# End of a second attention: output path and routing moved earlier, two banks for the products with v, fillers in the late slots

## The reference

```
x = x + attn_a(layernorm(x))      # 16 heads of 8, hyperbolic distances
x = x + ffn(layernorm(x))
x = x + attn_b(layernorm(x))      # 16 heads of 8, rotary, softmax(q k / sqrt(8)) v, projection
x = x + ffn(layernorm(x))

def ffn(x):                       # x: 2048 tokens x 128
    scores = sigmoid(x @ router_w.T); sfc = scores + e_bias          # 64 experts in 8 groups
    group_scores = top_k(sfc by group, 2).sum(-1)
    keep the 4 best groups, then the 8 best experts of those
    w = 2.5 * scores of the 8 / their sum                            # coef, zero elsewhere
    return sum_e (silu(x @ Wg_e) * (x @ Wu_e) * coef_e) @ Wd_e + shared expert
```

## Time and profile before

| what | value |
|---|---|
| median of 3 runs (lowest, highest) | 1089.32 us (1086.78, 1092.47) |
| profiled execution: own time, span | 1086.67 us, 1084.9 us |
| TensorE matmul busy | 971.3 us (90%) |
| VectorE busy | 959.2 us (88%) |
| ScalarE busy | 671.2 us (62%) |
| mean granted TensorE clock | 0.867 of full speed |

### The profile page before, as it was taken

One profiled execution on the slowest core, in us unless ns is written; L12 is line 12 of the kernel. 1 busy time (PEld: TensorE's weight loads), 2 busy tenths in 40 slices (PEclk: granted clock), 3 DMA queues, 4 the chain that ended last, 5 costly groups with the idle time before them and its releaser, 6 DMA issues. The chain is left out here.

```text
span 1084.9 us, 17540 instructions
## 1 busy us (share of the span) xinstructions
PE 971.3 (90%) x5387; PEld 694.7 (64%) x5387; DVE 959.2 (88%) x1447; ACT 671.2 (62%) x848; POOL 368.7 (34%) x266
## 2 busy tenths in 40 slices
PE   6767887878669999999999899899889999999997
PEld 4533444444347888888888555455568888888886
DVE  7799999999988999999999797987589999999997
ACT  4779999999934545445445554876544544545544
POOL 2054666667901433333331211111203333333330
PEclk9865555555669999999999998999789999999999
DMA  2000000000119555555550000112049555555521
GB/s 59 1 1 1 1 1 1 1 1 1 52 30 215 157 160 151 147 157 147 155 153 4 1 1 1 23 23 31 16 107 225 151 147 157 148 154 155 147 85 39
DMA packets 50711, 86.94 MB, mean 80 GB/s; under 512 B 20092, under 2 KB 33404, under 8 KB 50556
## 3 DMA queue, kind: packets, MB, share of 16 engines
q1 hardware_dynamic: 50664, 86.34, 30.6%
HBM read 83.33 MB, written 2.98 MB: 80 GB/s over the span
## 5 line engine op out<-in xcount | busy, mean ns | idle before, releaser
L1514 ACT ACTIVATE sg<-ps 128x512 f32<-128x512 f32 x264 | 156.8, 594 | 264.8 <-PE ps L523 263.2
L523 PE MATMUL ps<-xh,whi 128*128 128x512 f32 x528 | 206.2, 391 | 1.3 <-ACT b L1330 1.3
L523 PE MATMUL ps<-xl,whi 128*128 128x512 f32 x528 | 205.9, 390 | 0.0
L523 PE MATMUL ps<-xh,wlo 128*128 128x512 f32 x528 | 205.8, 390 | 0.0
L2329 DVE TENSOR_TENSOR hf<-sg,ps 128x512 f32<-128x512 f32 x264 | 170.3, 684 | 29.9 <-DVE hl L2336 24.4
L1727 POOL CAST whi<-wraw 128x384 fp32r<-128x384 f32 x66 | 66.3, 1004 | 370.2 <-PE ps L523 285.5
L1647 POOL TENSOR_TENSOR rr<-xr,rr 128x2048 f32<-128x2048 f32 x32 | 145.2, 4569 | 125.0 <-ACT rr L1305 71.2
L2336 DVE TENSOR_TENSOR hl<-hf,hh 128x1024 fp32r<-128x1024 f32 x132 | 178.2, 1350 | 0.8 <-DVE hf L2329 0.8
L2341 DVE TENSOR_TENSOR hf<-hf,cbc 128x1024 f32<-128x1024 f32 x128 | 157.6, 1231 | 13.4
L1542 ACT ACTIVATE hh<-hf 128x1024 fp32r<-128x1024 f32 x132 | 139.2, 1055 | 4.6 <-DVE hf L2341 4.6
L1729 POOL TENSOR_TENSOR wlo<-wraw,whi 128x384 fp32r<-128x384 f32 x66 | 116.3, 1762 | 5.3
(11 more groups left out here) (277 smaller groups left out, 1512.3 us busy)
## 6 DMA issues: line engine op xcount, KB each, us to landing
cbc<-routing_coefficients SPq DMA_DIRECT2D x256, 256.0 KB, 3.8
wraw<-in_wexp_dram SPq DMA_DIRECT2D x66, 192.0 KB, 2.7
X<-in_x_dram SPq DMA_DIRECT2D x4, 256.0 KB, 4.8
routing_coefficients<-cT SPq DMA_DIRECT2D x8, 128.0 KB, 2.3
out_dram<-X SPq DMA_DIRECT2D x4, 256.0 KB, 2.9
heads_by_row<-o_all SPq DMA_DIRECT2D x12, 72.0 KB
b_rows<-heads_by_row SPq DMA_DIRECT2D x12, 72.0 KB, 2.7
rope_in<-in_consts_dram SPq DMA_DIRECT2D x1, 512.0 KB, 3.4
```

The source lines that it names most:

```text
L523: return pe.matmul(o, l, r, start=start, stop=stop, **kw)
L1514: act.activation(sg[c % 2][:, :], bank(4 + 2 * (c % 2)), ACT.Silu).then_inc(s_sg, 1)
```

## The change

Five things are changed, all between slot 42 of the second attention and the start of the second expert loop.

- The output path of chunk 1 (`normalise`, `transposed`, `projected`, `residual`, `stats_of`) moves one to five slots earlier, and fillers are placed anew.
- The two `f_transposed` of half 0 move from U = 53 and 55 to V = 59 and 61 (U = 48 and 50), their copies from VectorE to ScalarE (`copy_xT`), and the logits from U = 56 and 57 to 53 and 54.
- The products with v of the last groups alternate between banks 6 and 2.
- `TAIL_FILL` adds one filler to most slots from U = 55 and two to each of the last three.
- Routing of half 0 is cut into pieces. Sigmoids go by group. `route_masked` to `route_coefs` of half 0 and its `lows` move out of `prepare_f` into `samples_b`, between the steps of chunk 3. `lows` of half 1 comes before its routing, not after. In `last_of_b` TensorE's order changes, and the last copy to `f_xT` goes from ScalarE to VectorE.

The diff, cut where helpers are only moved or renamed:

```diff
@@ -390,6 +391,21 @@
...
+        def logit_bank(f, i, g):
...
+            if f == 0:
+                return bank(spare(f, i, g) + 1)[:, 0:GTILES * E]
+            n, at = ((0, 0), (1, 0), (1, 0), (1, 1))[2 * i + g]
+            return bank(n)[:, at * GTILES * E:(at + 1) * GTILES * E]
...
+        def pair_bank(n):
+
+            return 2 if 2 * n >= LAST_PAIRS and n % 2 else 6
@@ -876,7 +892,8 @@
...
-            WAITS_FOR_PATH = {39: 4, 46: 3, 47: 4, 55: 4, 62: 3, 63: 4}
+            WAITS_FOR_PATH = {39: 4, 46: 3, 47: 4, 54: 4, 57: 2, 58: 3}
+            TAIL_FILL = {55: 1, 56: 1, 57: 1, 58: 1, 60: 1, 62: 1, 63: 1, 64: 2, 65: 2, 66: 2}
@@ -898,6 +915,8 @@
...
+                elif U in TAIL_FILL:
+                    keep_busy(shifted_bank(2 * U) if U <= 61 else 0, TAIL_FILL[U])
@@ -920,10 +939,12 @@
...
-                if s in (4, 6):
-                    pe.wait_ge(s_oTs, B + s // 2 - 1)
-                elif s in (5, 7):
-                    pe.wait_ge(s_ores, B + s // 2 - 1)
+                if s == 4:
+                    pe.wait_ge(s_oTs, B + 1)
+                elif s in (5, 6):
+                    pe.wait_ge(s_ores, B + s - 4)
+                elif s == 7:
+                    pe.wait_ge(s_fxT, GROUPS + 2)
@@ -950,8 +971,11 @@
...
                 if C % 2 == 0 and half == 0 and C >= 2:
-                    pe.wait_ge(s_bev, C // 2)
-                last = pv(vt, s, c, wr[:, C % CHUNKS, :], bank(6)[:, C % 2 * N:(C % 2 + 1) * N], (half,))
+                    if C == LAST_PAIRS:
+                        pe.wait_ge(s_mx, 2 * B * UNITS - 2)
+                    else:
+                        pe.wait_ge(s_bev, C // 2 if C < LAST_PAIRS else C // 2 - 1)
+                last = pv(vt, s, c, wr[:, C % CHUNKS, :], bank(pair_bank(C // 2))[:, C % 2 * N:(C % 2 + 1) * N], (half,))
@@ -993,32 +1017,35 @@
...
-                if V in (38, 54):
-                    c = (V - 38) // 16
+                if V in (38, 53):
+                    c = (V - 38) // 15
                     pe.wait_ge(s_q2, 2 * (V // UNITS))
                     pe.wait_ge(s_on, B + c + 1)
                     transposed(c, 7)
-                elif V in (43, 59):
+                elif V in (43, 55):
                     pe.wait_ge(s_q2, 2 * (V // UNITS))
-                    projected((V - 43) // 16, 7)
+                    projected((V - 43) // 12, 7)
+                elif V == 59:
+                    pe.wait_ge(s_q2, 2 * (V // UNITS))
+                    f_transposed(1, 0, 0)
+                elif V == 61:
+                    pe.wait_ge(s_fxT, GROUPS + 1)
+                    f_transposed(1, 0, 1)
             def b_tail_step(U):
                 if U == 53:
                     pe.wait_ge(s_mx, 2 * B * UNITS - 1)
-                    f_transposed(1, 0, 0)
-                elif U == 55:
+                    logits(1, 0, 0)
+                elif U == 54:
                     pe.wait_ge(s_mx, 2 * B * UNITS)
-                    f_transposed(1, 0, 1)
-                elif U == 56:
-                    logits(1, 0, 0)
-                elif U == 57:
                     logits(1, 0, 1)
                 elif U == 59:
                     pe.wait_ge(s_q2, 2 * B)
                     pe.wait_ge(s_on, B + 3)
                     transposed(2, 7)
                 elif U == 61:
+                    pe.wait_ge(s_sc, lap(1, 0, 1))
                     projected(2, 1)
@@ -1026,30 +1053,23 @@
                 pe.wait_ge(s_bev, 2 * B)
                 token_major(0, 2)
                 token_major(1, 4)
+                keep_busy(6, 2)
+                pe.wait_ge(s_oTs, B + 3)
+                f_transposed(1, 1, 0)
+                keep_busy(6, 2)
                 pe.wait_ge(s_on, B + 5)
                 transposed(3, 2)
-                keep_busy(4, 3)
-                projected(3, 3)
-                f_transposed(1, 1, 0)
                 pe.wait_ge(s_ores, B + 3)
                 logits(1, 1, 0)
-                keep_busy(4, 4)
+                projected(3, 3)
+                keep_busy(4, 6)
                 f_transposed(1, 1, 1)
                 keep_busy(4, 3)
                 logits(1, 1, 1)
...
             def normal_bank(f, i, g):
-                return spare(f, i, g) if f == 0 else (0, 1, 7, 6)[2 * i + g]
...
+                return spare(f, i, g) if f == 0 else (7, 7, 7, 6)[2 * i + g]
@@ -1415,27 +1435,32 @@
...
-                    if U in (27, 43):
-                        o_transposed_b((U - 27) // 16, 7)
-                    elif U == 37:
-                        f_norm_rstd(1, 0)
-                    elif U == 52:
-                        f_norm_rstd(1, 1)
-                    elif U == 58:
-                        logit_exps(1, 0)
+                    if U in (27, 42):
+                        o_transposed_b((U - 27) // 15, 7)
+                    elif U in (37, 47):
+                        f_norm_rstd(1, (U - 37) // 10)
+                    elif U in (48, 50):
+                        copy_xT((U - 48) // 2)
+                    elif U in (54, 55):
+                        logit_exps(1, 0, (U - 54,))
                     elif U == 60:
                         o_transposed_b(2, 7)
                     elif U == B * UNITS:
                         f_norm_rstd(1, 2)
...
+            def copy_xT(g):
+                act.wait_ge(s_fxnT, GROUPS + g + 1)
+                act.activation(f_xT[g][:, :], bank(7), ACT.Copy).then_inc(s_fxT, 1)
+                act.wait_ge(s_fxT, GROUPS + g + 1)
+                f_high(g)
@@ -1451,26 +1476,14 @@
...
             def last_of_b():
-                act.wait_ge(s_fxT, GROUPS + 2)
-                f_high(0)
-                f_high(1)
+                copy_xT(2)
                 o_transposed_b(3, 2)
-                act.wait_ge(s_fxnT, GROUPS + 3)
-                act.activation(f_xT[2][:, :], bank(7), ACT.Copy).then_inc(s_fxT, 1)
                 f_norm_rstd(1, 3)
-                act.wait_ge(s_fxT, GROUPS + 3)
-                f_high(2)
                 f_norm_apply_group(1, 3)
                 act.preload_act_table_set("sigmoid_and_others")
-                act.wait_ge(s_fxnT, 2 * GROUPS)
-                act.activation(f_xT[3][:, :], bank(6), ACT.Copy).then_inc(s_fxT, 1)
-                scores(1, 1)
                 act.wait_ge(s_fxT, 2 * GROUPS)
                 f_high(3)
...
+                scores(1, 1)
@@ -1707,7 +1719,8 @@
...
                     elif s == 5:
                         f_norm_apply_b(0)
-                f_norm_apply_b(1)
+                    elif s == 6:
+                        f_norm_apply_b(1)
@@ -2026,12 +2039,13 @@
             def prepare_f(f):
                 if f == 1:
-                    route_experts(f, 0)
+                    lows(f, 1)
                 route_bests(f, 1)
                 route_groups(f, 1)
                 route_masks(f, 1)
                 route_experts(f, 1)
-                lows(f, 1)
+                if f == 0:
+                    lows(f, 1)
@@ -2278,37 +2292,41 @@
...
-                    if V in (37, 53):
-                        normalise((V - 37) // 16)
-                    elif V in (44, 60):
+                    if V in (37, 52):
+                        normalise((V - 37) // 15)
+                    elif V in (44, 55):
                         if V == 44:
                             dve.wait_ge(s_pbx, 1)
-                        residual((V - 44) // 16, 7)
-                    elif V in (45, 61):
-                        stats_of((V - 45) // 16)
-                    elif V == 52:
-                        offset(0)
-
-                offset(1)
-                copy_xT(0, 0)
+                        residual((V - 44) // 11, 7)
+                    elif V in (45, 56):
+                        stats_of((V - 45) // 11)
+                    elif V in (50, 59):
+                        offset((V - 50) // 9)
+
+                lows(1, 0)
                 shift(B - 1, 0)
+                marks(1)
+                sigmoids(1, 0, 0)
                 shift(B - 1, 1)
-                copy_xT(1, 1)
-                marks(1)
                 normalise(2)
-                sigmoids(1, 0)
+                sigmoids(1, 0, 1)
                 route_bests(1, 0)
-                route_groups(1, 0)
                 residual(2, 1)
                 stats_of(2)
+                route_groups(1, 0)
+                offset(2)
                 route_masks(1, 0)
                 normalise_last(0)
                 normalise_last(1)
-                offset(2)
+                route_masked(1)
                 residual(3, 3)
                 stats_of(3)
-                lows(1, 0)
+                route_marked(1)
                 offset(3)
+                route_weights(1, 0)
+                route_sums(1)
+                copy_xT(3, 6)
+                route_coefs(1, 0)
```

More of the change, by code:

```diff
@@ L39 @@
 AHEAD = UNITS + 3
+LAST_PAIRS = 26
 CR_GRP, CR_SCR = 2, 16
@@ L391, in shifted_bank, with spare @@
             return 3 + h % 3
+        def spare(f, i, g):
```

(39 more changed lines are left out.)

## The result

The changed kernel takes 1097.01 us (median of 6 runs, 1095.32 to 1099.58), the kernel before 1087.89 (1086.72 to 1092.47) beside it: ratio 1.0072, 95% interval 1.0054 to 1.009. It is slower, where I forecast 1084.7 and at most 1089.5. The profiled spans are 1095.0 and 1084.9 us. (The ratio is estimated over all runs and need not be the quotient of the medians.

What follows compares the result with a forecast made beforehand. Expert matmuls close the chain, so the start of routing of half 1 was taken to set the end. Gains 4.7 + 0.3 - 0.5 + 0.1 = 4.6 us off the median 1089.32 gave 1084.7; 8-in-10 range 1080.5 to 1089.5.

Steps and rivals of the forecast that it cites:

- Routing of half 0 and its `lows` leave the chain ... at no gain beyond the above: Before routing of half 1: moving these pieces out gains nothing more, since they hid the wait for the scores.
- D: Rival: logits in slots 53 and 54 make the clock fall sooner than 763; at 759.6 it gives 1095.7; chance 0.05.
- My clock reading: TensorE's fall to 1.2 GHz at 763 was put down to sparse work and not one long gap.
- The stretch to the last product: Last maxima's transposes to last product: clock 5.5, banks 1.1, transposes 1.1, fillers -3.0, together a gain of 4.7 us.
- A: The forecast case: the clock stays at 2.4 GHz until the last product; chance 0.66, range 1081.5 to 1087.5.
- The fillers: `TAIL_FILL`'s 13 fillers, ahead of the last product, were to cost 3.0 us, with bounds of -3.6 and -2.0.
- Both waits of bank 6: Two waits of 0.57 for the copy out, at 755.48 and 763.32, were to go: gain 1.1 us.
- my 5.5: Gain from 763.32 to the last product if the clock holds at 2.4 GHz; 0 if it doesn't.
- Slots 42 to 52: Transposes, copies and chunk 1's output path moved here: gain of 0.3 us, with bounds of -0.7 and +1.0.
- rival B: The clock holds but ScalarE becomes the bound in slots 48 to 52: gain 2.4, time 1086.9, chance 0.14.
- `last_of_b`: Last product to routing of half 1: -0.5, or -0.7 at low clock; pause before last transposes grows from 2 to 4.
- Last `lows`: The last `lows` (1.3) leaves its place behind the last coefficients, so VectorE's first expert products come sooner: gain 0.1 us.

Runs made afterwards that it cites:

- e1: The changed kernel with `lows(1, 0)` alone moved behind `route_bests` of half 0: 1087.74 us, ratio to before 0.9991.
- e9: The kernel before plus two VectorE subtractions right behind the last maxima, both operands in SBUF, result overwritten later: 1096.82 us, ratio 1.0079.
- e11: The kernel before plus two VectorE subtractions right behind the last maxima, one operand from PSUM, result overwritten later: 1090.12 us, ratio 0.9999.
- e10: e8 with `lows` of half 1 back behind its routing and `last_of_b` in its old order: 1082.99 us, ratio to before 0.9963.
- e8: e1 without `TAIL_FILL`: 1084.07 us, ratio to before 0.9963.
- e5: The kernel before with only the second bank for every other late group of products with v: 1088.51 us, ratio 0.999.
- e3: The changed kernel with three more fillers in each of slots 53 and 54: 1090.69 us, ratio to before 1.0015.
- e2: The changed kernel without `TAIL_FILL`: 1094.39 us (1082.64 to 1098.98 over ten runs), ratio to before 1.0019.

## Why the prediction was wrong

**The step that failed** is "Routing of half 0 and its `lows` leave the chain ... at no gain beyond the above". I costed `lows(1, 0)` only at the place it left and never at the place it came to. There it is issued 0.15 ahead of GpSimd's cast, behind which TensorE's transposes are queued. I had put that at nothing. Price in the profile: 0.87 for the split and 29.52 - 21.16 = 8.4 for the clock; in the time 0.8%, some 9 us, by the ratios (1.0072 against 0.9991 for e1), and 7.4 by the medians of e9 and its kernel before (1096.82 and 1089.44).

**The rivals.** The outcome is near D's number (1095.7, chance 0.05), an early fall of the clock, but D's mechanism was wrong: e1 has the same logits in slots 53 and 54 and 1.00 throughout. That the time came out near D's number was luck. My clock reading was about sparse work in general, and I put the danger at the thin logits, not at pauses that the change could lengthen. The range left D out.

**The stretch to the last product.** With the held split gone (e1), the forecast 4.7 measured 24.95 - 21.16 = 3.8. The clock held (A right). The fillers cost 3.5 and not 3.0, nearly the bound of 3.6. Both waits of bank 6 are gone. The base of this sum was one execution: e11, with before's code and two hidden instructions, fell at 764 as well but was back at 2.4 GHz by 771 and not 777, and ended 22.76 after the transposes where before had 24.95. So how long the clock stays down, and with it my 5.5, differs between executions of nearly the same kernel.

**Slots 42 to 52.** Forecast +0.3; e1 has 28.92 from transposes to transposes, before 28.32: -0.6, within the bounds. The changed kernel shows rival B's mechanism in small: behind the copies in slots 48 and 50, TensorE waits for ScalarE (timeline of TensorE):
```profile
749.48 0.35 PE L539 MATMUL ps<-b_kt,b_qt 32*128 32x256 f32 x1 [0.48 <-ACT wr L1432]
...
753.07 0.35 PE L539 MATMUL ps<-b_kt,b_qt 32*128 32x256 f32 x1 [0.49 <-ACT wr L1432]
```

**`last_of_b`.** Forecast -0.5, and -0.7 if the clock is low at the logits. Measured: 16.38 before, 16.99 after, -0.6, logits at 1.2 GHz (1.80). Right, and so was that the pause before the last transposes would grow from 2 to 4 (2.10 and 4.19) with the clock down behind it (0.73 in the window from 795 to 800). The old order is shorter in the profiles, though, by 0.45 (16.69 in e10, 17.14 in e8) to 1.85.

**Last `lows`.** Forecast +0.1; measured -0.8 from the coefficient transposes to the end (279.0 and 279.8). This can't be put down to the change. e5, e9 and e11 have before's code in this stretch and took 281.5, 281.4 and 281.5, and e8, with the new place of `lows`, took 278.8. The experts' first products on VectorE began 6.1 behind those transposes, 0.3 sooner than before, and one of them then met GpSimd's split of the weights. In VectorE's timeline of the changed kernel:
```profile
829.22 1.53 DVE L2354 TENSOR_TENSOR hl<-hf,hh 128x1024 fp32r<-128x1024 f32 x1
...
833.71 2.04 DVE L2354 TENSOR_TENSOR hl<-hf,hh 128x1024 fp32r<-128x1024 f32 x1
```
and in GpSimd's:
```profile
832.79 1.88 POOL L1742 TENSOR_TENSOR wlo<-wraw,whi 128x384 fp32r<-128x384 f32 x1
```
Such a product takes 1.22 to 1.53 elsewhere. Here it runs until 835.75, which is 1.08 behind the end of GpSimd's subtraction. It looks like the same block the other way round, but I only argue this; no run took it apart. Nor does it explain the stretch: e5 and e11, with before's order, have such a product of 2.04 too, and e9 has none at 281.4. What makes the 2.5 us between runs of equal code stays open.

**Taken together,** with the failed step taken back (e1) the forecast of 4.6 would still have been too high. From mark to mark, e1's profile against before's: 1.1 later ahead of the change, 0.6 later up to the last transposes, 3.8 sooner to the last product, 0.6 later to routing of half 1 (16.98), 2.5 later to the end (which same-code runs show too). That makes 1.0 later for the span (1085.9 and 1084.9), while e1's median is 1.09 below that of before (1087.74 and 1088.83), within what can't be told from no change. Before's profiled execution was one of its short ones. The parts that the change itself moves, 3.8 - 0.6 - 0.6, make 2.6.

## What to carry to other kernels

Work out the cost of a moved instruction at the place it comes to, and not only at the one it leaves. Look in the other engines' timelines for what starts within its duration there, and who waits for that; a VectorE operation with two SBUF inputs beside a short GpSimd operation on the path was not free here, and one PSUM input (e11) or a later place (e1) made it so. Where a stretch hangs on the clock, find the pauses that stand ahead of each fall, ask what would lengthen them, and try the removal of a pause before fillers: here it gave 9 us, and 3.5 us of fillers could then go. And follow a gain of one engine to the next wait: of e5's 6.0 us at the last product 2.7 were left at the routing that follows.

## What the runs showed that I had not expected

- A 1.30 us pair of VectorE instructions costs 7 to 9 us, some 0.87 directly and the rest by the clock (8.4 in the profile of the changed kernel against e1's), which comes back only after 20 us at 1.2 GHz (756.4 to 776.9).
- One operand from PSUM in place of SBUF sets GpSimd free: cast pair 0.35 against 1.22.
- A pause of 0.97 (after) or 1.31 (e9) ahead of thin logits was followed by the fall, while e3 with the split as late and dense work in its stead, e1 and e8 without a pause kept 1.00. A pause of 1.13 in slot 42 was followed by 0.50 in e3's profile and not in e1's, at the same code, and two of ten executions of e2 show no loss behind the held cast, so the same pause does not always bring it. The change lengthened this earlier pause too (it was 0.68 before), by moving `normalise` and `transposed` of chunk 1 a slot earlier. TensorE in before, in e1 and in e3:
```profile
733.77 0.63 PE L985 MATMUL ps<-cst,b_otok 128*128 128x128 f32 x4 [0.68 <-DVE b_otok L2240]
733.66 0.63 PE L1009 MATMUL ps<-cst,b_otok 128*128 128x128 f32 x4 [1.13 <-DVE b_otok L2254]
734.20 1.09 PE L1009 MATMUL ps<-cst,b_otok 128*128 128x128 f32 x4 [1.13 <-DVE b_otok L2254]
```
- Executions of one kernel differ by where the clock falls elsewhere: 0.67 in e5 and 1.00 in the kernel before at 640 to 645 us, at the same code, stand beside 2.2 us at the next mark.
